# Tables of task order of their own for the first and the last of sixteen images, in an attention kernel on one core

## What is computed

```python
wp = normalize_weight(w_proj)[:, :, 0, 0] / fan_in      # 1536 x 512
wo = normalize_weight(w_out)[:, :, 0, 0] / fan_in       # 512 x 512
h = jnp.einsum('oc,bcn->bno', wp, xf)
q, k, v = jnp.split(h.reshape(B, N, n_heads, 3 * d_k), 3, axis=-1)   # 8 heads of 64
q, k, v = pixnorm(q) * scale, pixnorm(k) * scale, pixnorm(v)
attn = jax.nn.softmax(jnp.einsum('bihd,bjhd->bijh', q, k), axis=2)
res = jnp.einsum('bijh,bjhd->bihd', attn, v).reshape(B, N, C)
res = jnp.einsum('oc,bnc->bon', wo, res)
return (a_c * x + b_c * res) / div                      # a_c = 0.7, b_c = 0.3
```

## Time and profile before

| what | before |
| --- | --- |
| median of 3 runs | 2993.76 us (2993.70 to 2994.16) |
| the profiled execution, its own time | 2993.77 us |
| its span, first to last instruction | 2992.0 us |
| TensorE busy | 2934.9 us, 98% |
| VectorE busy | 2582.7 us, 86% |
| ScalarE busy | 2381.6 us, 80% |
| GpSimd busy | 456.2 us, 15% |
| granted TensorE clock, mean | 1.00 (2.4 GHz) |

### The profile page before, as it was taken

One profiled execution on the slowest core, in us unless ns is written; L12 is line 12 of the kernel. 1 busy time (PEld: TensorE's weight loads), 2 busy tenths in 40 slices (PEclk: granted clock), 3 DMA queues, 4 the chain that ended last, 5 costly groups with the idle time before them and its releaser, 6 DMA issues.

```text
span 2992.0 us, 85444 instructions
## 1 busy us (share of the span) xinstructions
PE 2934.9 (98%) x36928; PEld 2014.0 (67%) x36928; DVE 2582.7 (86%) x3197; ACT 2381.6 (80%) x2993; POOL 456.2 (15%) x678
## 2 busy tenths in 40 slices
PE   7999999999999999999999999999999999999997
PEld 5676666766667667676666766666666666766664
DVE  6998888988889888898888988888898888988896
ACT  6887778878778778787787878788787778878785
POOL 0210121101211111112111211012110121101210
PEclk9999999999999999999999999999999999999999
DMA  3233414233242332333323333332422424233234
GB/s 99 49 55 67 90 32 109 49 82 76 44 96 52 78 79 50 87 62 79 69 58 78 62 80 67 68 72 58 97 56 63 91 39 107 51 70 88 35 77 100
DMA packets 459531, 211.04 MB, mean 71 GB/s; under 512 B 407954, under 2 KB 407954, under 8 KB 459154
## 3 DMA queue, kind: packets, MB, share of 16 engines
q1 hardware_dynamic: 459152, 205.58, 32.3%
HBM read 71.30 MB, written 33.55 MB: 35 GB/s over the span
## 4 chain that ended last, share of the span: by engine, by line
PE 78%; DVE 8%; POOL 5%; ACT 4%; issue 3%; DMA 3%; SPq 0%; ACTq 0%; DVEq 0%; POOLq 0%
PE ps_pv L930 20%; PE ps_score L909 18%; PE ps_dense L887 11%; PE ps_dense L889 10%; PE ps_dense L891 10%; DVE probs L722 4%; PE ps_dense L946 3%; PE ps_dense L948 2%; PE ps_dense L947 2%; DMA x_raw<-in_x 2%; POOL rs_t L369 1%; POOL rs_t L367 1%; POOL rs_t L371 1%; ACT e_tile L528 1%; ACT probs L535 1%
## 5 line engine op out<-in xcount | busy, mean ns | idle before, releaser
L722 DVE TENSOR_TENSOR probs<-e_tile,probs 128x1024 f16<-128x1024 f32 x1024 | 1241.3, 1229 | 71.0 <-ACT probs L535 64.8
L528 ACT ACTIVATE e_tile<-ps_score,shift 128x1024 f32<-128x1024 f32 x1024 | 1106.0, 1117 | 234.4 <-PE ps_score L909 135.2
L930 PEld LDWEIGHTS ps_pv<-v_pair,probs 128*128 128x128 f16 x24576 | 772.0, 98 | 187.4 <-issue 108.6
L930 PE MATMUL ps_pv<-v_pair,probs 128*128 128x65 f16 (+1 forms) x24576 | 821.5, 193 | 7.2 <-DVE probs L722 5.6
L909 PE MATMUL ps_score<-qkT 64*128 64x512 f16 x6144 | 753.9, 378 | 4.0 <-ACT e_tile L528 3.7
L887 PE MATMUL ps_dense<-wpT_hi,x_hi 128*128 128x512 f32 x1536 | 621.1, 404 | 1.8 <-DVE wpT_lo L793 1.5
L889 PE MATMUL ps_dense<-wpT_lo,x_hi 128*128 128x512 f32 x1536 | 600.0, 391 | 0.0
L891 PE MATMUL ps_dense<-wpT_hi,x_lo 128*128 128x512 f32 x1536 | 599.2, 390 | 0.0
L535 ACT ACTIVATE probs<-e_tile 128x1024 f16<-128x1024 f32 x512 | 542.6, 1060 | 21.4 <-PE ps_pv L930 2.1
L909 PEld LDWEIGHTS ps_score<-qkT 64*128 64x128 f16 x6144 | 257.0, 94 | 363.3 <-issue 90.7
L713 DVE CAST probs<-e_tile 128x1024 f16<-128x1024 f32 x512 | 359.4, 702 | 68.3 <-PE ps_pv L930 65.7
(11 more groups left out here) (50 smaller groups left out, 1737.0 us busy)
## 6 DMA issues: line engine op xcount, KB each, us to landing
x_raw<-in_x SPq DMA_DIRECT2D x128, 256.0 KB, 3.3
x_res<-in_x SPq DMA_DIRECT2D x128, 256.0 KB, 3.9
out<-x_res SPq DMA_DIRECT2D x128, 256.0 KB, 2.5
arena<-in_w_proj SPq DMA_DIRECT2D x24, 128.0 KB, 2.9
qkT<-arena SPq DMA_TRANSPOSE x128, 4.7
resT<-res_split SPq DMA_TRANSPOSE x128, 3.6
arena<-in_w_out SPq DMA_DIRECT2D x1, 1024.0 KB, 5.7
```

Source lines behind the costliest of these rows:

```text
L528: act.activation(e_tile[:, t % E_BUFS, :, :], ps_score[:, t % 2, :, :], ACT.Exp, bias=shift[:, 0:1], scale=1.0 / (QK_UP * QK_UP)).then_inc ...
L722: dve.tensor_tensor(probs_of(b, t, 1), e_tile[:, t % E_BUFS, :, :], probs_of(b, t, 0), ALU.subtract).then_inc(probs_low, 1)
L930: mm = pe.matmul(ps_pv[:, h, o:o + n], probs_of(b, t, part)[:, h, queries], v[:, cols], start=(j == 0 and it == 0 and part == 0 and cols.s ...
```

## The change

The tables are gathered in three dictionaries: STEADY for images 1 to 14, FIRST for image 0, LAST for image 15. STEADY holds the old common numbers times 16 (`TICKS` goes from 64 to 1024 for each slot) and nothing else new, except that both bank tables swap 0 and 1 throughout. FIRST holds a whole first image with its weights' tasks; LAST a whole last image. `timeline` sorts all moments of all images and calls the tasks in that order. The wait for a bank is now kept while the program is written: `take_bank` remembers who took the bank last.

```diff
-TICKS = 64
+TICKS = 1024
-PROJ_AT = (-1850, -1834, -1450, -1294, -1230, -1189, -1128, -1125, -955, -639, -604, -602, -41, 173, 236, 264,
-    930, 931, 934, 1421, 1714, 1715, 1716, 1860)
...
-PROJ_BANK = (1, 0, 1, 0, 1, 0, 1, 0, 1, 0, 1, 0, 1, 0, 1, 0, 1, 0, 1, 0, 1, 0, 1, 0)
-OUT_BANK = (1, 0, 1, 0, 1, 0, 1, 0)
...
+STEADY = {
...
+    "PROJ_AT": (-29600, -29344, -23200, -20704, -19680, -19024, -18048, -18000, -15280, -10224, -9664, -9632,
+        -656, 2768, 3776, 4224, 14880, 14896, 14944, 22736, 27424, 27440, 27456, 29760),
...
+    "PROJ_BANK": (0, 1, 0, 1, 0, 1, 0, 1, 0, 1, 0, 1, 0, 1, 0, 1, 0, 1, 0, 1, 0, 1, 0, 1),
+    "OUT_BANK": (0, 1, 0, 1, 0, 1, 0, 1),
+}
...
-        def timeline(eng, task, steady, opening):
-
-
-            span = SLOTS * TICKS
-
-            def body(b, prev=True, cur=True, nxt=True):
-                for s in range(span):
-                    if prev and s + span <= LAST_TICK:
-                        task(b - 1, s + span, steady)
-                    if cur:
-                        task(b, s, steady)
-                    if nxt and s - span >= FIRST_TICK:
-                        task(b + 1, s - span, steady)
-
-            for s in range(-span, 0):
-                task(0, s, opening)
-            body(0, prev=False)
-            for b in range(1, B - 1):
-                body(b)
-            body(B - 1, nxt=False)
-            body(B, cur=False, nxt=False)
+        def tables(b):
+
+            return FIRST if b == 0 else LAST if b == B - 1 else STEADY
+
+        def timeline(task, names):
+
+
+            plans = [{name: at(tables(b).get(table, ())) for name, table in names.items()} for b in range(B)]
+            moments = {(SLOTS * TICKS * b + tick, b, tick) for b in range(B) for found in plans[b].values()
+                       for tick in found}
+            for _, b, tick in sorted(moments):
+                task(b, tick, plans[b])
...
-            def bank_free(b, s, bank):
...
+            bank_left = {}
+
+            def take_bank(bank, emptied, count):
+
+                if bank in bank_left:
+                    pe.wait_ge(*bank_left[bank])
+                bank_left[bank] = (emptied, count)
...
-                bank = PROJ_BANK[n]
-                bank_free(b, PROJ_AT[n], bank)
+                bank = tables(b)["PROJ_BANK"][n]
+                take_bank(bank, proj_copied, 24 * b + n + 1)
```

More of the change, by code:

```diff
@@ L574, in _ @@
             act.wait_ge(consts_set, CONSTS)
-            steady = dict(exp=at(EXP_AT),
-                          cast=at(HIGH_P_AT),
-                          square=at(SQUARE_AT),
-                          copy=at(COPY_AT),
-                          high_v=at(HIGH_V_AT),
-                          high_qk=at(HIGH_QK_AT),
-                          high_res=at(HIGH_RES_AT),
-                          finish=at(FINISH_AT),
-                          high_x=at(HIGH_X_AT))
-            opening = dict(exp=at(FIRST_EXP_AT),
-                           cast=at(FIRST_HIGH_P_AT),
-                           square=at(FIRST_SQUARE_AT),
-                           copy=at(FIRST_COPY_AT),
-                           high_v=at(FIRST_HIGH_V_AT),
-                           high_qk=at(FIRST_HIGH_QK_AT),
-                           high_res=at(FIRST_HIGH_RES_AT),
-                           finish=at(FIRST_FINISH_AT),
-                           high_x=at(FIRST_HIGH_X_AT),
-                           w_square=at(W_SQUARE_AT),
-                           w_high=at(W_HIGH_AT))
-            def task(b, s, when):
-                if when is opening:
-                    for m in when["w_square"].get(s, ()):
-                        square_weights(m)
-                    for m in when["w_high"].get(s, ()):
-                        high_weights(m)
+            names = dict(exp="EXP_AT",
+                         cast="HIGH_P_AT",
+                         square="SQUARE_AT",
+                         copy="COPY_AT",
+                         high_v="HIGH_V_AT",
+                         high_qk="HIGH_QK_AT",
+                         high_res="HIGH_RES_AT",
+                         finish="FINISH_AT",
+                         high_x="HIGH_X_AT",
+                         w_square="W_SQUARE_AT",
+                         w_high="W_HIGH_AT")
+            def task(b, s, when):
+                for m in when["w_square"].get(s, ()):
+                    square_weights(m)
+                for m in when["w_high"].get(s, ()):
+                    high_weights(m)
                 for t in when["exp"].get(s, ()):
@@ L828, in task @@
-            def task(b, s, when):
-                if when is opening:
-                    for c in when["w_norm"].get(s, ()):
-                        norm_weights(c)
-                    for m in when["w_scale"].get(s, ()):
-                        scale_weights(m)
-                    for m in when["w_low"].get(s, ()):
-                        low_weights(m)
+            names = dict(take="TAKE_AT",
+                         low_res="LOW_RES_AT",
+                         add="ADD_OUT_AT",
+                         reduce="REDUCE_AT",
+                         seed="SEED_AT",
+                         scale="SCALE_AT",
+                         low_v="LOW_V_AT",
+                         low_qk="LOW_QK_AT",
+                         low_x="LOW_X_AT",
+                         cast="HIGH_P_AT",
+                         low_p="LOW_P_AT",
+                         w_norm="W_NORM_AT",
+                         w_scale="W_SCALE_AT",
+                         w_low="W_LOW_AT")
@@ L836, in task @@
+            def task(b, s, when):
+                for c in when["w_norm"].get(s, ()):
+                    norm_weights(c)
+                for m in when["w_scale"].get(s, ()):
+                    scale_weights(m)
+                for m in when["w_low"].get(s, ()):
+                    low_weights(m)
                 for u in when["take"].get(s, ()):
@@ L962, in _ @@
             pe.wait_ge(consts_set, CONSTS)
-            steady = dict(score=at(SCORE_AT),
-                          attend=at(ATTEND_AT),
-                          proj=at(PROJ_AT),
-                          out=at(OUT_AT))
-            opening = dict(score=at(FIRST_SCORE_AT),
-                           attend=at(FIRST_ATTEND_AT),
-                           proj=at(FIRST_PROJ_AT),
-                           out=at(FIRST_OUT_AT),
-                           w_turn=at(W_TURN_AT))
+            names = dict(score="SCORE_AT",
+                         attend="ATTEND_AT",
+                         proj="PROJ_AT",
+                         out="OUT_AT",
+                         w_turn="W_TURN_AT")
             def task(b, s, when):
-                if when is opening:
-                    for m in when["w_turn"].get(s, ()):
-                        turn_weights(m)
+                for m in when["w_turn"].get(s, ()):
+                    turn_weights(m)
                 for m in when["attend"].get(s, ()):
```

283 lines of the change are left out of this document (148 added, 135 removed), and 45 rows, old and new, of tables (EXP_AT, FIRST, HIGH_P_AT, LAST).

## The result

| | before | after |
| --- | --- | --- |
| median of 12 runs each, on one chip | 2994.11 us (2990.79 to 2995.84) | 2987.47 us (2985.61 to 2988.67) |
| the profiled execution, its own time | 2993.77 | 2986.36 |
| its span | 2992.0 | 2984.6 |

The ratio is 0.9978, 95% interval 0.9971 to 0.9985: 6.6 us or 0.22% faster, just over what can be told from no change. The forecast was 3.2 us faster.

The account below looks back on a forecast made before the run. TensorE was taken as nearly always busy, so reordering could win only idle time: 2993.77 + 1.0 (start) - 1.4 (end of attention) - 2.8 (tail) = 2990.6 us. The range was 2984.0 to 2998.0.

Parts of the forecast that it names:

- the three places: Where time could change: a chained start, the last image's attention end set by VectorE, and a tail of chained transfers.
- The tail: After the last subtraction of probabilities: earlier finish0, stores and loads save 2.8 us, bounds -1.3 and -4.
- Rival (d): Tail: slower landings, as stores and loads overlap more, take its gain; 2993.4 us; chance 0.18 together with rival (c).
- End of attention: Last image: two tasks fill VectorE's 2.29 us wait before the cast of step 20; -1.4 us, bounds 0 and 5.6.
- rival (b): Last image: the last group's norm on GpSimd runs slowly, everything behind 6 us late; 2998.0 us, chance 0.10.
- The start: First image: uncovered table load and later x pieces delay the first projection; +1.0 us, ends -0.5 and +4.
- the step through the landing of x piece 3: Start: the piece's later load lands at 19.85, so the first projection starts at 21.95, 1.0 later.
- The norm of group 1: First image, on GpSimd: starts near 86.7 instead of 79.51 and ends near 94.
- Rival (c): Start: group 1's norm stays slow, scale4 at 96.5, attend7 3.6 late; 2993.2 us; chance 0.18 together with Rival (d).
- The table load without its cover: Start, ScalarE: the 1.28 us load now follows the weights' wait, a loss of 0.35 instead of a 0.93 gain.
- The middle: From image 0's score7 to image 14's attend29: costed at nothing; forecast wrong if it differs by over 1 us.
- rival (a): Last image: more VectorE waits go, low_p35 5.6 earlier, and the start costs nothing; 2985.4 us, chance 0.26.

Follow-up runs that it names:

- e2: The changed program with only the first image's new order, the last image keeping the common one; 2995.12 us, ratio 1.0001 to the kernel before.
- e3: The changed program with only the last image's new order, the first image keeping the old one; 2989.05 us, ratio 0.9978 to the kernel before.
- e4: All old orders except five tasks in the last image's tail, which take the new order; 2992.27 us, ratio 0.9991 to the kernel before.
- e5: The changed kernel with the old order in the last image's tail alone; 2991.68 us, ratio 0.9988 to the kernel before.
- e1: The changed program, banks swapped, with the old order of every task; 2994.70 us, ratio 0.9998 to the kernel before.
- e10: The changed kernel with low_res1 and reduction 21 put back behind the cast of step 20 in the last image; 2989.89 us, ratio 0.9984.
- e11: The changed kernel with projection 23, its square, reduction and seed2 late again in the last image, so its last norm starts late; 2992.24 us, ratio 0.9990.
- e6: The changed kernel with a tiny ACTIVATE ahead of ScalarE's wait for the weights, so the table load runs early; 2988.25 us, ratio 0.9975.
- e7: The changed kernel with x pieces 0 and 1 ahead of the weights again and pieces 2 and 3 loaded behind the first weights; 2987.99 us, ratio 0.9975.
- e8: The changed kernel with a buffer for each of the last image's eight residual pieces, all loaded before turn_res4; 2985.59 us, ratio 0.9967.

## Why the prediction was right and wrong

**Right: the three places.** By e2 to e5 the gain is made in the attention and in the tail of the last image, each by itself, and e1 has no other.

**The tail, right in mechanism and nearly in size.** Counted from the end of low_p63, I had finish0 at 2.94, store1 5.34, load2 5.74, load3 7.69, load4 12.54; measured are 2.92, 5.32, 5.70, 7.75 and 12.68. The term was -2.8. The pair measured -3.2 and the mean over eleven executions -2.6: load4 was 2.9 earlier in the pair, and the rest came in the last two rounds, in the one execution with the shortest landing of piece 4's store. Rival (d), no gain, is refuted.

**End of attention: the step that failed.** The term was -1.4, the stretch measured -2.5, and its cause was another. I wrote that the two tasks put into the 2.29 us wait were "1.4 us which VectorE needn't do later". The wait did go, but it had slack behind it: VectorE was to wait for the norm at scale8 anyway. e10 prices those two tasks at 0.36. What gave the 2.5 us is the norm that starts earlier: against the change, e11 loses 2.7. I had seen seed2 move ahead, from 2881 to near 2877.6, but took it up only as a danger, in rival (b), and not as the gain that it was. My own scale8, "near 2888.7", stood 2.9 us ahead of the 2891.64 of the kernel before, and 2.9 is what scale8 then gained in its stretch; it was never put into the sum. The row that should have told me is the norm's end in the earlier trace rows, followed at once by the scaling that waited for it: a wait of only 1.05, but the last one before VectorE was as good as full to the end (busy 64.34 of the 65 us from 2894.48 on).

Rival (b) had its mechanism right and its outcome wrong: the end does hang on this norm. It took 11.5 us in the change (10.5 before, 9.5 in e11, where VectorE waits more), under the 14 with which it would have ended as late as before. The rival's price was wrong as well. It counted 6 us from my own 2888.7 and added them to the time of the kernel before; against that kernel's 2891.64, an end near 2894.7 is 3 us late. The Trainium skill (SBUF — State Buffer, "Who interferes with whom") says that a VectorE operation with two inputs in SBUF and a GpSimd operation that reads SBUF lock each other out. The trace agrees: the product of L444, the same operation in each of the norm's three rounds, takes 0.65, 1.22 and 0.32 in the rows above. It took 1.22 beside the first of these rows of VectorE, which reads two tiles in SBUF, and 0.32 beside the second, which reads ps_pv:

```profile
2880.00 2.49 DVE L780 TENSOR_TENSOR probs<-e_tile,probs 128x1024 f16<-128x1024 f32 x2
...
2883.41 0.69 DVE L792 TENSOR_TENSOR res<-ps_pv,inv_sum 128x512 f32<-128x512 f32 x1
```

Slower by 1.0 in all, the norm still ended 4.5 us earlier, since it began 5.5 earlier (counted in its stretch, 2.9 and 3.9).

**The start, mis-sized in both directions.** The term was +1.0. The first projection came 1.75 later instead of 1.0: the weights landed at 8.36 and not at 8.10, and the step through the landing of x piece 3 (19.85) was not the limit; two subtractions in front of the last low part were. But at attend8 only 0.4 was left in this pair and 0.6 on the mean of four and six executions, and e2 shows no cost in the whole (1.0001). On the same means the first projection is 1.6 late, so 0.9 is made up between the two: TensorE's idle time in that stretch is 0.9 to 1.8 us in the four executions with the old start and 0.3 to 0.5 in the six with the new one. Part of the low mean of the four is e4, 0.9 ahead of the next, in which none of the first matmuls was slow. TensorE had no new idle of over 0.5 us at the fifth weight tile or at proj4, as forecast. The norm of group 1 was as I had it: 86.76 to 94.31, scale4 at 94.41, where I let it end near 94. Rival (c) did not come. The table load without its cover was real: 0.63 at the first square by the timeline, and e6 takes 1.2 off the first projection. The Trainium skill (ScalarE: Activation LUTs, "What ACT_TABLE_LOAD costs") adds a drain to a switch of sets and comes to 2.66 us. Here the first ACTIVATE begins 1.30 after the load does, so the trace doesn't agree for a program's first load.

**The middle, right in the sum and wrong as a test.** I had said that I would be wrong if the middle differed by over 1 us. It differs by 2.0 in the profiles. But its length in e1, which has the order of before, is 2673.58, and in e7 2669.64 and e8 2673.63, which have the order of the change there: the spread of single executions is 4.0 us with one order. (The nine with the new start are 1.4 shorter on the mean than the four with the old one, which this spread doesn't let me call a gain.) One wait that varies with it is TensorE's for ScalarE's copy of a projection, in front of the output projection; from 160 to 2790 us in the kernel after, and then in e8:

```profile
PE ps_dense L989 <- ACT arena L564: 17.7, 24, 1.6
```

```profile
PE ps_dense L986 <- ACT arena L558: 19.9, 25, 1.9
```

It makes 2.2 of the 3.8 between the two. Over all thirteen executions it is 17.5 to 21.2 us and goes with the length of the middle: the length less this wait is 2652.1 to 2652.6 in twelve of them, and 2653.7 in e8. So nearly all of the spread is this one wait; why it is longer in one execution than in another with the same order stays open. The medians of e1 and e2 show no gain of the middle, with intervals that reach some 2.7 us either way.

**The sum.** +0.4, -2.5 and -3.2 by the pair are -5.3 us, +0.6, -2.5 and -2.6 by the means over all executions -4.5; the medians say -6.6, with an interval from -8.7 to -4.5. What the medians have beyond the traces' terms is not accounted for. Against +1.0, -1.4 and -2.8 the start was 0.4 to 0.6 too dear, the attention 1.1 too small and the tail right to 0.4 either way. So the forecast had about half of the gain. It called it no change that can be told, with a chance of 0.61, and the measured 2987.47 lies just under the 2987.8 from which it is one, where I had 0.30; that it lies in the range at all is owed to the room made for rival (a). Rival (a), 2985.4, came nearer in size than the forecast; its cause, low_p35 5.6 earlier, did not come: low_p35 came 1.9 earlier in its stretch (114.74 against 116.60 from the start of attend28).

## What to carry to other kernels

Before you credit work put into a wait, look for the next wait of the same engine behind it: what is gained ahead of that wait is only slack. The last wait before an engine is busy to the end decides, however short it is, and what moves it is the start of the chain it waits for, here a norm of 14 small operations on GpSimd that began 3.9 us earlier in its stretch, took 1.0 longer and gave 2.5.

In a tail of load, add, scale, store with two buffers, issue the stores before the loads that depend on them; with a buffer for every piece the transfers leave the path, and TensorE's 12 matmuls for each piece are the bound (e8: 4.0 to 5.1 us in the traces of the tail, 2.4 to 2.7 in the medians). A difference of 2 us in one stretch of two single profiles, with the same order in it, means nothing until a second execution has been looked at.

## What the runs showed of the hardware

- The compiler's table load stands behind the wait of the first ACTIVATE. With an instruction ahead of it that waits for nothing large, it ran at 0.73 instead of 8.36 (e6).
- The last image's attention is nearly the same in every execution (scale8 at 94.79 or 94.80 behind attend28 in the seven with its new order), while the middle of 14 images varies by 4.0 us and the tail of transfers by 1.1 (24.87 to 26.00).
- The 14 operations of one norm took 7.6 us at 86.76 and 11.5 us at 2875.53: the time depends on what VectorE does beside it. The last operation alone took 0.32 beside a waiting VectorE (after) and 1.18 beside a subtraction (e10).
